# Normed rows of pairs four to eight: split by rows and turned by two DMA transposes instead of by TensorE

## The reference, cut to what matters

```python
# x: (16, 64, 1024); ctx_4096: (16, 1024, 1024); float32
x = x + xattn(layernorm(x), ctx_4096, scales, zero points)   # fake-quantised matmul
x = x + attn(layernorm(x), qkv_w, qkv_b, out_w, out_b)       # 32 heads of 32, rope, causal
x = x + ffn(layernorm(x), W, bias, A, Bf, coeffs, scales)    # dense plus low-rank update

def attn(h, qkv_w, qkv_b, out_w, out_b):
    q, k, v = split(h @ qkv_w + qkv_b)        # 1024 -> 3 x 1024
    q, k = rope(q), rope(k)
    p = softmax(q k^T / sqrt(32) + causal mask)
    return (p v) @ out_w + out_b
```

## Time and profile before

| | |
|---|---|
| median of 3 runs | 614.53 us (614.21 to 615.3) |
| profiled execution | 614.66 us, span in the trace 612.8 us |
| TensorE busy | 590.3 us, 96% |
| VectorE busy | 467.2 us, 76% |
| ScalarE busy | 293.3 us, 48% |
| GpSimd busy | 125.4 us, 20% |
| DMA | 111.31 MB, 182 GB/s mean |

### The profile page before, as it was taken

How to read it: one execution, slowest core, us unless ns; L and a number is a source line. 1 busy time by engine, 2 the same in 40 slices (tenths; PEclk the granted TensorE clock), 3 DMA queues, 4 the chain that set the end, 5 groups by cost and what they waited for, 6 DMA issues and landing times.

```text
span 612.8 us, 13105 instructions
## 1 busy us (share of the span) xinstructions
PE 590.3 (96%) x4929; PEld 296.2 (48%) x4929; DVE 467.2 (76%) x932; ACT 293.3 (48%) x360; POOL 125.4 (20%) x173
## 2 busy tenths in 40 slices
PE   3899999999999999999999999999999999989998
PEld 1464454455445444554455445555445554434445
DVE  6899998788767966787676868667964789866771
ACT  5987795865456445543654564456231243210110
POOL 4000010000265225513541453446000000000000
PEclk9999999999999999999999999999999999999999
DMA  8999996861366265507622562464231043257461
GB/s 321 387 386 361 397 357 233 258 232 70 139 197 217 70 230 185 202 0 274 240 103 80 198 241 97 150 217 147 103 137 35 1 150 126 87 105 178 129 154 70
DMA packets 51586, 111.31 MB, mean 182 GB/s; under 512 B 16474, under 2 KB 16858, under 8 KB 51552
## 3 DMA queue, kind: packets, MB, share of 16 engines
q1 hardware_dynamic: 37744, 104.35, 47.9%
q10 hardware_dynamic: 13536, 5.95, 4.5%
q0 software_dynamic: 272, 0.55, 0.2%
HBM read 99.30 MB, written 8.39 MB: 176 GB/s over the span
## 4 chain that ended last, share of the span: by engine, by line
PE 79%; DVE 14%; DMA 3%; issue 3%; ACT 1%; SPq 0%; DVEq 0%
PE dense L1360 15%; PE dense L1361 14%; PE dense L1362 14%; PE turn L1351 5%; PE dense L1554 4%; PE dense L1556 4%; PE dense L1555 4%; DVE wq L932 4%; PE cross L1424 3%; PE cross L1409 3%; PE score L1515 3%; PE dense L1570 2%; PE score L1541 2%; DMA wq<-x_scratch 2%; PE cross L1601 1%
## 5 line engine op out<-in xcount | busy, mean ns | idle before, releaser
L1360 PE MATMUL dense<-wq,xn_h 128*128 128x512 f16 x400 | 152.2, 380 | 2.7 <-DMA xn_l<-spare 2.3
L1361 PE MATMUL dense<-wq,xn_h 128*128 128x512 f16 x400 | 151.6, 379 | 0.0
L1362 PE MATMUL dense<-wq,xn_l 128*128 128x512 f16 x400 | 151.6, 379 | 0.0
L802 POOL TENSOR_TENSOR acc<-code,acc 128x256 int32<-128x256 int32 x140 | 104.1, 772 | 114.2 <-ACT code L378 114.2
L378 ACT ACTIVATE code<-raw,cst,qc 128x1024 uint8<-128x1024 f32 x72 | 87.2, 1237 | 14.0 <-DMA raw<-in_ctx 13.3
L1360 PEld LDWEIGHTS dense<-wq,xn_h 128*128 128x128 f16 x400 | 39.0, 98 | 52.3 <-issue 15.9
L1362 PEld LDWEIGHTS dense<-wq,xn_l 128*128 128x128 f16 x400 | 39.2, 98 | 47.2
L1361 PEld LDWEIGHTS dense<-wq,xn_h 128*128 128x128 f16 x400 | 39.2, 98 | 34.6
L378 ACT ACTIVATE code<-lnt,cst,qc 128x1024 uint8<-128x1024 f32 x32 | 39.6, 1238 | 28.8 <-DMA lnt<-in_ctx 28.3
L989 DVE SCALAR_TENSOR_TENSOR at<-cst,score 128x512 f32<-128x512 f16 x24 | 16.4, 683 | 39.9 <-PE score L1515 39.9
L1554 PE MATMUL dense<-wo,rope 128*128 128x512 f16 x112 | 42.5, 379 | 0.8 <-DVE rope L1019 0.8
(11 more groups left out here) (221 smaller groups left out, 1040.0 us busy)
## 6 DMA issues: line engine op xcount, KB each, us to landing
raw<-in_ctx SPq DMA_DIRECT2D x72, 512.0 KB, 4.4
lnt<-in_ctx SPq DMA_DIRECT2D x32, 512.0 KB, 4.2
wo<-in_ctx SPq DMA_DIRECT2D x16, 512.0 KB, 9.2
wo<-in_qkv_w SPq DMA_DIRECT2D x12, 512.0 KB, 11.9
wq<-in_qkv_w SPq DMA_DIRECT2D x8, 512.0 KB, 11.7
x_scratch<-xa SPq DMA_DIRECT2D x8, 512.0 KB, 3.1
wq<-x_scratch SPq DMA_DIRECT2D x8, 512.0 KB, 4.5
wq<-in_ctx SPq DMA_DIRECT2D x7, 512.0 KB, 11.7
```

Of the source, the lines that this page charges most:

```text
L802: ins = pool.tensor_tensor(sums[:, cols], words[:, cols], acc_from.to_broadcast([P, half]) if c < 2 else sums[:, cols], ALU.add)
L1360: pe.matmul(bank[:, :], a_h[:, k, :], w_hi, start=(k == 0 and not started), stop=False)
L1361: pe.matmul(bank[:, :], a_h[:, k, :], w_lo, start=False, stop=False)
L1362: ins = pe.matmul(bank[:, :], a_l[:, k, :], w_hi, start=False, stop=(k == KC - 1 and not last))
```

## The change

For pairs four to eight (i = 3 to 7) the normed rows are no longer turned by TensorE. VectorE computes one more factor, minus mean times reciprocal deviation, into `nw[:, 3:4]` and still writes `lnt`. ScalarE computes the high half by rows straight from `xb` with scale and bias, into `x_hl[0]`, half of the softmax buffer `pr`. VectorE subtracts it from `lnt` into `x_hl[1]`. ScalarE issues a DMA transpose of each into `xn_h` and `xn_l`. The first product of pairs three to eight does its 16 matmuls with `xn_h` first, and waits for the low half only then. The last count of `s_xt` (the release of `lnt`) now comes from VectorE's subtraction. The loop on ScalarE is written out, so that its body is there for each i; the other loops stay.

```diff
+            def rows_turned(i):
+                act.wait_ge(s_xfac, i - TILED + 1)
+                act.activation(x_hl[0], xb[:, :], ACT.Identity, scale=nw[:, 0:1], bias=nw[:, 3:4]).then_inc(s_xrowh, 1)
+                act.wait_ge(s_xrowh, i - TILED + 1)
+                act.wait_ge(s_qkv, 6 * i)
+                act.dma_start_transpose(xn_h[:, :, :], x_hl[0]).then_inc(s_xturnh, 16)
+                act.wait_ge(s_xt, 2 * i + 2)
+                act.dma_start_transpose(xn_l[:, :, :], x_hl[1]).then_inc(s_xturnl, 16)
...
                 c_high(i, 1)
-                x_high(i + 1, 0)
-                x_high(i + 1, 1)
                 if late:
+                    x_high(i + 1, 0)
+                    x_high(i + 1, 1)
                     value_bias()
+                else:
+                    rows_turned(i + 1)
...
-            with act.Fori(2, PAIRS - 2) as i:
+            for i in range(2, PAIRS - 2):
                 next_pair(i, True)
...
+                if tiled(i):
+                    dve.wait_ge(s_xturnh, 16 * (i - 2))
                 dve.tensor_scalar(d16, q8_tile, QMID, None, ...).then_inc(s_a, 1)
...
                 else:
+                    if tiled(i):
+                        dve.tensor_scalar(nw[:, 3:4], mv[:, 0:1], nw[:, 0:1], -1.0, ALU.mult, ALU.mult).then_inc(s_xfac, 1)
                     dve.tensor_scalar(lnt[:, :], x_rows(i)[:, :], mv[:, 0:1], nw[:, 0:1], ALU.subtract, ALU.mult).then_inc(s_xn, 1)
+
+            def x_rows_low(i):
+                dve.wait_ge(s_xn, i + 1)
+                dve.wait_ge(s_xrowh, i - TILED + 1)
+                dve.tensor_tensor(x_hl[1], lnt[:, :], x_hl[0], ALU.subtract).then_inc(s_xt, 2)
...
+                elif j == 0 and not isinstance(i, int) or i > 1 and j == 0:
+                    for k in range(KC):
+                        for w in (wq_h, wq_l):
+                            pe.matmul(D[0][:, :], xn_h[:, k, :], w[:, k, n * NT:(n + 1) * NT], ...)
+                    pe.wait_ge(s_xturnl, 16 * (i - 1))
+                    for k in range(KC):
+                        pe.matmul(D[0][:, :], xn_l[:, k, :], wq_h[:, k, n * NT:(n + 1) * NT], ...)
+                    both_biases()
...
-                pe.wait_ge(s_xl, 2 * i + 2)
+                if isinstance(i, int) and i == 1:
+                    pe.wait_ge(s_xl, 2 * i + 2)
+                else:
+                    pe.wait_ge(s_pte, 4 * i)
+                    pe.wait_ge(s_xturnh, 16 * (i - 1))
...
-                if ahead:
+                if late:
                     x_turn(i + 1)
-                else:
+                if not ahead:
                     merge(6)
                     merge(7)
                 project(i, 0, 1)
```

More of the change, by code:

```diff
@@ L126, in build @@
         d16 = pr[:, 0, :].bitcast(F16)
+        x_hl = [pr[:, n, :].bitcast(F16) for n in range(2)]
         acc_words = acc[:, :].bitcast(I32).rearrange("p (b n) -> p b n", b=2)
@@ L190, in build @@
         s_xl = sem("s_xl")
+        s_xfac = sem("s_xfac")
+        s_xrowh = sem("s_xrowh")
+        s_xturnh = sem("s_xturnh")
+        s_xturnl = sem("s_xturnl")
         s_u8 = sem("s_u8")
@@ L921, in norm2 @@
                 else:
+                    if tiled(i):
+                        dve.tensor_scalar(nw[:, 3:4], mv[:, 0:1], nw[:, 0:1], -1.0, ALU.mult, ALU.mult).then_inc(s_xfac, 1)
                     dve.tensor_scalar(lnt[:, :], x_rows(i)[:, :], mv[:, 0:1], nw[:, 0:1], ALU.subtract, ALU.mult).then_inc(s_xn, 1)
+            def x_rows_low(i):
+                dve.wait_ge(s_xn, i + 1)
+                dve.wait_ge(s_xrowh, i - TILED + 1)
+                dve.tensor_tensor(x_hl[1], lnt[:, :], x_hl[0], ALU.subtract).then_inc(s_xt, 2)
             def x_low(i, e):
                 dve.wait_ge(s_xh, 2 * i + e + 1)
+                done, count = (s_xl, 1) if i < 2 else ((s_xturnh, s_xturnl)[e], 16)
                 dve.tensor_tensor(xn_l[:, 4 * e:4 * e + 4, :].rearrange("p k t -> p (k t)"), T[e][:, :],
-                                  xn_h[:, 4 * e:4 * e + 4, :].rearrange("p k t -> p (k t)"), ALU.subtract).then_inc(s_xl, 1)
+                                  xn_h[:, 4 * e:4 * e + 4, :].rearrange("p k t -> p (k t)"), ALU.subtract).then_inc(done, count)
             def weight_lo(j):
@@ L1135, in next_pair @@
                 c_low(i, 1)
-                x_low(i + 1, 0)
-                x_low(i + 1, 1)
+                if late:
+                    x_low(i + 1, 0)
+                    x_low(i + 1, 1)
+                else:
+                    x_rows_low(i + 1)
                 out_evac(i, 0)
@@ L1472, in qkv @@
                     dense(D[j % 2], xn_h, xn_l, wq_h, wq_l, n * NT, False, s_qkv, between, due)
+                elif j == 0 and not isinstance(i, int) or i > 1 and j == 0:
+                    for k in range(KC):
+                        for w in (wq_h, wq_l):
+                            pe.matmul(D[0][:, :], xn_h[:, k, :], w[:, k, n * NT:(n + 1) * NT], start=(k == 0 and w is wq_h), stop=False)
+                    pe.wait_ge(s_xturnl, 16 * (i - 1))
+                    for k in range(KC):
+                        pe.matmul(D[0][:, :], xn_l[:, k, :], wq_h[:, k, n * NT:(n + 1) * NT], start=False, stop=False)
+                    both_biases()
                 else:
```

## The result

| | before | after |
|---|---|---|
| median of 5 runs each, on one chip | 614.65 us (614.21 to 615.3) | 619.79 us (618.05 to 621.86) |
| profiled execution | 614.66 us, span 612.8 | 619.79 us, span 618.0 |
| ratio after to before | | 1.0083, 95% interval 1.0069 to 1.0097 |

The kernel is slower by 5.1 us; the forecast was faster by 4.1. The range, up to 613.9, does not hold the time.

The account below looks back on a forecast made before the run. TensorE, busy 96% of the span, was taken as the bound. Saving 0.82 us a pair, 4.1 in all, from 614.66 gave 610.6, and 610.4 us since the runs' median lies 0.13 lower; range 609.4 to 613.9.

Parts of the forecast that it names:

- What is taken off TensorE: Eight transposes at each of five pair ends leave TensorE, 0.87 us each time, 4.35 us in all.
- First place, the third projection piece: Third projection piece waits for `c_low(i, 1)`, delayed about 0.15 us; cost 0 to 0.1 us a pair, 0.05 taken.
- Second place, the high half: At the next pair's first matmul: high half lands 3.3 to 4.5 us after issue, over a microsecond in hand.
- the rival on it: High half lands late at each pair's first matmul, stopping TensorE; full price 623.2 us, half the stop 616.8; chance 0.10.
- Third place, the low half: Low half, wanted 16 matmuls into the first product, 7.6 us after issue, lands in time; cost 0.
- the bound: Low half's latest landing, all traffic moved first: high 1.8, low 1.8, loads 3.9, fixed 1.5 us from 273.1, giving 282.1.
- What else moves: the codes and `a_high`: Transposes delay a load by up to 1.8 us, hence ScalarE's codes and `a_high`; 1.4 us in hand, cost 0.
- the rival was real: Delayed loads make codes and `a_high` late, stopping TensorE in the second product: 2.0 us in all, 612.4 us; chance 0.11.
- the slower one: High half lands late at each pair's first matmul; 6.9 us after issue makes it slower by over 0.2%; chance 0.10.
- Nothing gained: VectorE's chain through `c_low` holds TensorE where the turn stood, if 0.9 us later than forecast: 614.5 us; chance 0.09.
- codes late: Transposes delay loads beyond their own 1.8 us, `a_high` comes late, TensorE stops in the second product: 612.4 us; chance 0.11.

Follow-up runs that it names:

- nothing turned: The changed kernel without its ten DMA transposes, TensorE multiplying the rows that pair three left: 612.02 us, ratio 0.9955 to the kernel before.
- loads behind with `a_high` ahead: The changed kernel with context loads held until the low half landed and ScalarE's two `a_high` copies before the pair's fourth code: 612.64 us, ratio 0.9968.

## Why the prediction was wrong

**What is taken off TensorE** was right: 0.87 us forecast, 0.88 in every distance that nothing disturbed (57.25 to 56.37, and 58.30 to 57.42).

**First place, the third projection piece,** was right: TensorE waits there as before, 0.8 us in five times, none longer than 0.2. ScalarE's pass with scale and bias took 1.24 us where I had taken 1.06 from the earlier trace rows; it lies beside other work.

**Second place, the high half,** was right: it landed 3.1 to 3.2 us after its issue, just below the 3.3 to 4.5 that I took, and never stopped TensorE. The Trainium skill speaks, for the rival on it, of transfers that interleave whoever issued them (DMA: Bandwidth & Descriptors, Issuing engines are not separate DMA queues). It was the right warning at the wrong half: the high half's 1.4 us of lead kept it out of the loads' way.

**Third place, the low half, is the step that failed.** I put its landing at 282.1 at the latest and its cost at 0. The landing took up to 11.4 us where 7.6 to 7.9 were to be had, and TensorE stood still for 4.3 us. Three errors are in it. First, the median and the slowest of the earlier trace rows came from transposes with little beside them, and I passed to three loads with only a bound to cover it. Second, the bound's terms were misread. The 1.8 us for each transpose came from a stretch in which SyncE stored a result too (593 to 597 moved 0.79 MB, the two transposes are 0.52); alone they take 2.7 us together. The 3.9 us for the loads left out what moved before 276 and after 280; three loads alone took 4.2 (before, 389 to 396). And the copy and the fourth load, which SyncE issues some five us after the low half, were not in it at all. Third, and most of it, the bound added times that each kind takes alone, as if company cost nothing. In pair seven the bound's own terms give 386.89 + 1.5 + 1.8 + 1.8 + 3.9 = 395.9, just in time for TensorE at 396.1. With the terms read rightly, 2.7 and 6.1 us from 388.0 on, before which nothing moves, it is 396.8, a stop of 0.7; the low half landed at 399.66. The rest, 2.9 us, goes with SyncE's packets taking 9.5 us where 6.1 are their time alone.

The runs show the step from both sides: with the loads held back the landing is 3.1 us, with one beside it 5.1 to 5.7; and with the deadline later the same landings of 5.7 to 11.3 us cost 0.5 us instead of 4.3.

The Trainium skill (DMA: Bandwidth & Descriptors, Queues, rings and completion order) says that each DMA engine takes turns between the queues that have work for it, a packet from each. That goes with what is seen, but no run tests it: the two transposes are 2112 packets of some 250 bytes, three loads 432 of some 3600 on average. That the packets of the loads then take half as long again as alone is not in that rule, and the runs here show it.

**Not in the forecast at all: the clock.** After the stop of 3.62 us the granted clock was 0.50 for another 5.5 us, and pair seven lost another 2.8 us by it. After the stops of up to 1.8 us in the last stage of before it stayed at 1.00. The same low matmuls in pair four, behind a stop of 0.67 us, took 1.90 us, against 3.59. A stop of this length can cost more than its length; in the experiments stops of 2.3 and 2.4 us did too.

**What else moves: the codes and `a_high`.** Forecast as 1.4 us in hand and cost 0; that held in the changed kernel, where TensorE never waited for `a_high`. But the rival was real: each way of getting the loads out of the low half's way brought it out, 1.6 us, 3.1 us. A smaller thing I had not seen: VectorE's codes took 1.23 us beside GpSimd's sums (L898, and L819 on GpSimd, pair five, after):

```profile
283.17 3.28 POOL L819 TENSOR_TENSOR acc<-code,acc 128x256 int32<-128x256 int32 x4 [0.83 <-ACT code L383]
...
284.64 1.23 DVE L898 TENSOR_SCALAR rope<-at,ab 128x1024 uint8<-128x1024 f32 x1
```

where this code takes 0.81 in before, in each of the four pairs. The distances to pairs five and six, where it is slow, are 0.5 and 0.2 us over 56.37. That it is the reason is not shown: nothing turned has 57.17 and 56.74 there with 0.81 in each pair (its wait at `rope` L1005 is that instruction taking 1.01 us instead of 0.69), and loads behind with `a_high` ahead has 1.10 in pair seven and 56.37.

**The last stage** was forecast unchanged and took 1.5 us more. That is also why no version reached the 610.4 us forecast: in the pairs the best one has 4.0 of the 4.1 us, and with before's last stage its profiled execution of 612.49 would be 610.65. In the changed kernel it is mostly TensorE waiting longer for that stage's own transposes (3.6 us of waits in all against 2.3); why they are late has no cause shown.

**The rivals:** the slower one had the right mechanism, a transposed half that waits for the traffic, but it was put at the high half, which leads the loads by 1.4 us, and not at the low half, which is issued with them. Nothing gained and codes late did not happen in this kernel.

## What to carry to other kernels

A transfer that must be there by a deadline is to be priced in the company it will have, not alone; where loads are issued in the same instant, take several times its time alone, or hold them back and look at who waits for them. Moving work that another engine does to the DMA engines pays only if both are done: here holding the loads alone gained nothing, holding them and moving two copies ahead of one code gained 0.3%. And a stop of TensorE of two to four microseconds can cost more than its length, by the clock that follows.

## What the runs showed of the hardware

- A DMA transpose of 128x1024 float16 (256 KB) within on-chip memory landed 3.1 to 3.3 us after its issue with no load beside it, 5.1 to 5.7 with one load of 512 KB, 6.3 to 11.4 with three. It is 1056 packets of some 250 bytes. Two take 2.7 us of the DMA engines' time, some 194 GB/s, where loads alone move 374.
- Beside the two transposes 2.29 MB of loads and a copy took 9.5 us of the DMA engines' time, where 6.1 are their time alone (an estimate from 1.57 MB in 4.2 us); the transposes' own 2.7 us stayed. Single microseconds of that stretch show shares from 0.59 to 1.72.
- Issuing a transpose holds ScalarE's queue for 1.25 to 1.6 us as a rule; in the last stage of the kernels with rows split by rows one or two of twelve took 2.1 to 3.2 us.
- From 60 us on, a granted clock of 0.50 came 0.5 to 1.1 us after the end of stops of TensorE of 2.31, 2.40, 2.96 and 3.38 us, for some three us, and during one of 3.62 us, for seven. It did not come after stops of 2.35 and 3.08 us, nor after any of 1.8 us and less, nor after one of 3.84 us near the start of before (13.45 us).
- A pass of ScalarE over 128x1024 with scale and bias by partition took 1.24 us, a copy of the same width 1.06 us.
